# Three weight folds on TensorE in split fp32r products instead of f32, with the splitting on ScalarE and GpSimd

## The reference

```
Q = (x @ Wq), K = (ctx @ Wk), V = (ctx @ Wv)      # per batch, 8 heads of 256
score = Q K^T / sqrt(256); masked; attn = softmax(score)
out = (attn V) @ Wo + x
(out - mean) * rsqrt(var + 1e-5) * gamma + beta
```

## Time and profile before

| | us |
|---|---|
| median of 3 runs | 312.84 (312.39 to 313.38) |
| profiled execution | 312.59 |
| its span | 310.8 |
| TensorE busy | 304.6 |
| VectorE busy | 243.9 |
| ScalarE busy | 228.2 |
| GpSimd busy | 201.2 |
| granted clock | 1.00 |

### The profile page before, as it was taken

One profiled execution on the slowest core, in us unless ns is written; L12 is line 12 of the kernel. 1 busy time (PEld: TensorE's weight loads), 2 busy tenths in 40 slices (PEclk: granted clock), 3 DMA queues, 4 the chain that ended last, 5 costly groups with the idle time before them and its releaser, 6 DMA issues.

```text
span 310.8 us, 8035 instructions
## 1 busy us (share of the span) xinstructions
PE 304.6 (98%) x2570; PEld 298.0 (96%) x2570; DVE 243.9 (78%) x696; ACT 228.2 (73%) x615; POOL 201.2 (65%) x209
## 2 busy tenths in 40 slices
PE   8999999999999999999999999999999999999994
PEld 6898888999999999999999999999999999999994
DVE  0457778778998779787989879877988889877676
ACT  2546678768888687878887887868797797868760
POOL 1123476556868588857868487858878487857811
PEclk9999999999999999999999999999999999999999
DMA  7996444473354644574346543474455444543301
GB/s 248 367 404 257 138 137 153 144 218 114 95 167 144 208 154 135 175 249 139 114 147 190 185 148 118 164 232 135 135 172 181 155 141 147 166 149 124 84 2 68
DMA packets 48143, 51.32 MB, mean 165 GB/s; under 512 B 3584, under 2 KB 38144, under 8 KB 48128
## 3 DMA queue, kind: packets, MB, share of 16 engines
q1 hardware_dynamic: 47840, 50.61, 49.2%
q10 hardware_dynamic: 288, 0.52, 0.6%
HBM read 32.77 MB, written 18.35 MB: 164 GB/s over the span
## 4 chain that ended last, share of the span: by engine, by line
PE 96%; DMA 2%; DVE 1%; SPq 0%; POOLq 0%; issue 0%; POOL 0%
PE score_bank L346 25%; PE out_bank L346 19%; PE gL_bank L346 14%; PE tL_bank L346 13%; PE tU_bank L346 9%; PE gU_bank L346 7%; DMA wq_raw<-in_wqT 2%; PE spare_bank L346 1%; PE spare_bank L380 1%; PE tL_bank L380 1%; PE tL_bank L362 1%; PE tU_bank L362 1%; PE out_bank L386 1%; PE tU_bank L386 1%; PE spare_bank L362 0%; PE out_bank L362 0%
## 5 line engine op out<-in xcount | busy, mean ns | idle before, releaser
L1055 POOL TENSOR_TENSOR probs<-probs,inv_sum 128x512 f32<-128x512 f32 x64 | 66.7, 1043 | 63.1 <-DVE inv_sum L859 62.8
L651 ACT ACTIVATE probs<-neg_scores,neg_max 128x256 f32<-128x256 f32 x128 | 64.1, 502 | 32.3 <-DVE neg_max L848 32.3
L1098 POOL TENSOR_TENSOR pT_lo<-pT_raw,pT_hi 128x512 fp32r<-128x512 f32 x62 | 79.3, 1302 | 10.0 <-ACT pT_hi L607 10.0
L848 DVE CUSTOM_DVE_ANT_0 neg_scores<-score_bank,mask_bias 128x256 f32<-128x256 f32 x128 | 49.2, 422 | 6.7 <-PE score_bank L346 4.2
L869 DVE STREAM_TRANSPOSE squares<-probs 128x512 f32<-128x512 f32 x62 | 43.8, 706 | 0.3
L794 DVE TENSOR_TENSOR tL_lo<-tL_bank,tL_hi 128x512 fp32r<-128x512 f32 x30 | 20.8, 692 | 23.9 <-ACT tL_hi L607 23.9
L607 ACT ACTIVATE tL_hi<-tL_bank 128x512 fp32r<-128x512 f32 x30 | 17.9, 598 | 24.7 <-PE tL_bank L346 24.5
L607 ACT ACTIVATE pT_hi<-pT_raw 128x512 fp32r<-128x512 f32 x62 | 35.4, 623 | 0.0
L346 PE MATMUL gL_bank<-xT_hi,A_lo 128*128 128x256 f32 x128 | 35.3, 276 | 0.0
L346 PE MATMUL gL_bank<-xT_hi,A_hi 128*128 128x256 f32 x128 | 35.3, 276 | 0.0
L346 PE MATMUL gL_bank<-xT_lo,A_hi 128*128 128x256 f32 x128 | 35.3, 276 | 0.0
(11 more groups left out here) (192 smaller groups left out, 1010.7 us busy)
## 6 DMA issues: line engine op xcount, KB each, us to landing
scratch<-squares SPq DMA_DIRECT2D x31, 512.0 KB, 2.6
pT_raw<-scratch SPq DMA_DIRECT2D x124, 128.0 KB, 3.1
xT_raw<-in_xT SPq DMA_DIRECT2D x8, 256.0 KB, 3.2
ctxT_raw<-in_ctxT SPq DMA_DIRECT2D x8, 256.0 KB, 3.5
wo_raw<-in_wo SPq DMA_DIRECT2D x4, 512.0 KB, 14.8
x_res<-in_x SPq DMA_DIRECT2D x8, 256.0 KB, 3.0
out<-y SPq DMA_DIRECT2D x7, 256.0 KB, 2.7
wq_raw<-in_wqT SPq DMA_DIRECT2D x3, 512.0 KB, 7.6
```

Source lines behind the costliest of these rows:

```text
L651: nc.scalar.activation(probs[j % 2][:, n, :], neg_scores[:, n, :], ACT.Exp, bias=neg_max[:, n:n + 1], scale=-1.0, accum_out=row_sum[:, n:n ...
L848: nc.vector.tensor_tensor_reduce(out=neg_scores[:, n, :], in0=score_bank[hh][:, q, :], in1=mask_bias[:], scale=-SCALE, scalar=3.0e38, op0= ...
L1055: nc.gpsimd.tensor_tensor(probs[j % 2][:, rows, :], probs[j % 2][:, rows, :], inv, ALU.mult) \
L1098: nc.gpsimd.tensor_tensor(pT_lo[j % 2][:, k].rearrange("p hh (q i r) -> p (hh q) i r", q=QT, i=ROWS), pT_raw[j % 2][:, k].rearrange("p i n ...
```

## The change

The lower rows of fold 0 stay in f32. For pairs 1 to 3, wo (two heads, 128x512 each) and the lower 128 columns of wv (two heads, 128x256 each) are split into hi and lo: four ScalarE copies and four GpSimd subtractions a pair. They go into buffers that are idle at the time. The fold of the lower rows is 12 fp32r matmuls and stands behind the upper rows, which stay in f32; ScalarE and VectorE take the upper part first as well. SyncE's load of ctx moves from before the wv and wo loads to behind those of pair 1.

```diff
+        def wo_split(j, hh):
+            if j < PAIRS - 1:
+                return pT_hi[j - 1][:, hh], pT_lo[j - 1][:, hh]
+            return (gL_hi[:], gL_lo[:]) if hh == 0 else (gU[:], tL_hi[:])
+        def wv_split(j, hh):
+            if j < PAIRS - 1:
+                return by_half(CL_hi[:, 2 * j + 2 + hh, :]), by_half(CL_lo[:, 2 * j + 2 + hh, :])
+            return by_half(tL_lo[:, hh, :]), by_half((tU_hi, tU_lo)[hh][:])
+        def weight_parts(j, n):
+            tiles = slice((2 * j + n % 2) * DT, (2 * j + n % 2 + 1) * DT)
+            if n < 2:
+                return (wo_raw[:, tiles, :],) + wo_split(j, n)
+            return (wv_raw[:, tiles, 0:P],) + wv_split(j, n - 2)
...
@@ SyncE
-            load_ctx(0)
             for j in range(PAIRS):
                 ...
                 sp.dma_start(wo_raw[:, tiles], wo[:, tiles]).then_inc(o_weights_in[j], 16)
+                if j == 1:
+                    load_ctx(0)
@@ TensorE, fold_C (the f32 lower rows only for j == 0; the upper rows, then)
+                if j > 0:
+                    pe.wait_ge(weights_split, 4 * j)
+                    for hh in range(2):
+                        (v_hi, v_lo), (o_hi, o_lo) = wv_split(j, hh), wo_split(j, hh)
+                        pairs = []
+                        for d in range(DT):
+                            pairs += [(v_hi[:, d, :], o_hi[:, d, :]), (v_hi[:, d, :], o_lo[:, d, :]),
+                                      (v_lo[:, d, :], o_hi[:, d, :])]
+                        ins = split_products(lower[:, hh, :], pairs)
+                    ins.then_inc(C_product, 1)
@@ ScalarE
+            def weights_hi_part(j, n):
+                act.wait_ge(o_weights_in[j], 32)
+                raw, hi, _ = weight_parts(j, n)
+                hi_part(hi, raw).then_inc(weights_hi_done, 1)
...
+                if isinstance(t, int) and t == 0:
+                    weights_hi_part(1, 0)
+                    weights_hi_part(1, 1)
                 exponentials(t, j, heads=[0])
+                if isinstance(t, int) and t == 0:
+                    weights_hi_part(1, 2)
+                    weights_hi_part(1, 3)
                 ...
                 exponentials(t, j, heads=[1])
                 ...
                 for pair in folds:
                     C_hi_part(pair)
+                if isinstance(t, int) and t in (0, 1):
+                    for n in range(4):
+                        weights_hi_part(t + 2, n)
@@ GpSimd
+            def weights_lo_part(j, n):
+                pool.wait_ge(weights_hi_done, 4 * (j - 1) + n + 1)
+                raw, hi, lo = weight_parts(j, n)
+                lo_part(lo, raw, hi).then_inc(weights_split, 1)
...
+                if isinstance(t, int) and t == 0:
+                    weights_lo_part(1, 0)
+                    weights_lo_part(1, 1)
                 normalise_probs(t, j)
+                if isinstance(t, int) and t == 0:
+                    weights_lo_part(1, 2)
+                    weights_lo_part(1, 3)
+                    weights_lo_part(2, 0)
+                    weights_lo_part(2, 1)
                 if isinstance(t, int) and t == 1:
+                    weights_lo_part(2, 2)
+                    weights_lo_part(2, 3)
                     ctx_lo_part(b)
+                    weights_lo_part(3, 0)
+                if isinstance(t, int) and t == 2:
+                    weights_lo_part(3, 1)
+                    weights_lo_part(3, 2)
+                    weights_lo_part(3, 3)
                 ...
                 if j == 2 and not (isinstance(b, int) and b == B - 1):
                     xT_lo_part(b + 1)
```

More of the change, by code:

```diff
@@ L141, in attention_kernel, with pair_tiles, by_half @@
         pT_banks = [gL_bank, gU_bank]
+        def pair_tiles(j):
+            return slice(2 * j * DT, 2 * (j + 1) * DT)
+        def by_half(rows):
+            return rows.rearrange("p (d c) -> p d c", d=DT)
+        def wo_split(j, hh):
[11 more added lines that the diff above has]
+            return (wv_raw[:, tiles, 0:P],) + wv_split(j, n - 2)
         def places(name, t):
@@ L173, in attention_kernel @@
         A_split = sem("A_split")
+        weights_hi_done = sem("weights_hi_done")
+        weights_split = sem("weights_split")
         C_product = sem("C_product")
@@ L376, in fold_C @@
                 lower, upper = fold_C_banks(j)
[L377 to L382, removed]
+                if j == 0:
+                    for hh in range(2):
+                        h = 2 * j + hh
+                        for d in range(DT):
+                            ins = nc.tensor.matmul(lower[:, hh, :], wv_raw[:, h * DT + d, 0:P],
+                                                   wo_raw[:, h * DT + d, :], start=d == 0, stop=d == DT - 1)
+                    ins.then_inc(C_product, 1)
                 for hh in range(2):
@@ L622, in C_hi_part @@
                 act.wait_ge(C_product, 2 * j + 1)
-                hi_part(CL_hi[:, 2 * j:2 * j + 2, :], lower[:]).then_inc(C_hi_done, 1)
-                act.wait_ge(C_product, 2 * j + 2)
+                if j == 0:
+                    hi_part(CL_hi[:, 2 * j:2 * j + 2, :], lower[:]).then_inc(C_hi_done, 1)
+                    act.wait_ge(C_product, 2 * j + 2)
                 hi_part(CU_hi[:, j, :], upper[:, 0, :]).then_inc(C_hi_done, 1)
+                if j > 0:
+                    act.wait_ge(C_product, 2 * j + 2)
+                    hi_part(CL_hi[:, 2 * j:2 * j + 2, :], lower[:]).then_inc(C_hi_done, 1)
+            def weights_hi_part(j, n):
+                act.wait_ge(o_weights_in[j], 32)
+                raw, hi, _ = weight_parts(j, n)
+                hi_part(hi, raw).then_inc(weights_hi_done, 1)
             def ctxT_hi_part(b):
@@ L809, in C_lo_part @@
                 dve.wait_ge(C_hi_done, 2 * j + 1)
-                lo_part(CL_lo[:, 2 * j:2 * j + 2, :], lower[:], CL_hi[:, 2 * j:2 * j + 2, :]).then_inc(C_split, 1)
-                dve.wait_ge(C_hi_done, 2 * j + 2)
+                if j == 0:
+                    lo_part(CL_lo[:, 2 * j:2 * j + 2, :], lower[:], CL_hi[:, 2 * j:2 * j + 2, :]) \
+                        .then_inc(C_split, 1)
+                    dve.wait_ge(C_hi_done, 2 * j + 2)
                 lo_part(CU_lo[:, j, :], upper[:, 0, :], CU_hi[:, j, :]).then_inc(C_split, 1)
+                if j > 0:
+                    dve.wait_ge(C_hi_done, 2 * j + 2)
+                    lo_part(CL_lo[:, 2 * j:2 * j + 2, :], lower[:], CL_hi[:, 2 * j:2 * j + 2, :]) \
+                        .then_inc(C_split, 1)
             def lower_mask(b):
```

## The result

The changed kernel takes 313.88 us (median of 8 runs, 313.36 to 315.13), the kernel before 312.77 (8 runs): a ratio of 1.0037, interval 1.0022 to 1.0053. Slower, as forecast, but by 1.1 us where the forecast had 2.25 (2.3 on the median). The profiled execution took 313.88 with a span of 312.1, against 312.59 and 310.8: 1.3 us, nearly all of it there by the start of step 4's scores.

A forecast was written before the change was run, and what follows sets the result against it. TensorE, 98% busy, bounds the kernel, with VectorE's g loop and GpSimd's list close behind. Terms +1.92 - 0.44 + 0.27 - 0.44 + 0.55 - 0.44 + 0.83 = +2.25 us gave 314.84 profiled, 315.1 median; range 312.8 to 316.3.

The forecast's parts named there:

- the first stall: TensorE before step 1's scores: stands still 1.92 us, waiting for g delayed by the weight transfer; 0 to 2.4 by landing.
- the fold's saving: Lower fold on TensorE in steps 1 to 3: twelve fp32r matmuls in 1.38 us instead of 1.82, saving 0.44 each.
- step 1 with its fold, to step 2's scores: TensorE in step 1: fold saves 0.44 us, but VectorE's loop holds step 2's scores, giving back 0.27.
- step 2, to step 3's scores: TensorE in step 2: fold saves 0.44 us, but VectorE's loop holds step 3's scores, costing 0.55.
- wait for xT: Step 3's query products wait 0.83 us for xT's lower part, behind three weight parts on GpSimd in step 2.
- rest of step 3 with its fold: TensorE in step 3, apart from the xT wait: fold saves its full 0.44 us.
- This brings it 0.5 us forward: 22.0: Landing of pair 1's wo: moving ctx behind it brings it from 22.52 to 22.0 us; bounds 19.0 to 22.5.
- a first exponential before 22: Sign that would break the forecast, on ScalarE in step 0; the forecast had the first exponential near 23.0 us.
- would make 1.5: Pricing the twelve fold matmuls from the score products, 0.125 us apiece, gives 1.5 us; the forecast took 1.38.
- the loop holds there, as forecast: VectorE's g loop, periods 7.25 then 7.49 us, doesn't shrink with the fold; until step 3 TensorE can win only 0.24.
- Nothing is given back: From step 4's scores on TensorE sets the pace, so the whole +2.25 us stays to the end.
- the clock falls in the stall: Rival: TensorE, standing 1.92 us before step 1, drops to 1.2 GHz, costing up to 6.9 us more, 322; chance 0.03.

The follow-up runs named there:

- the changed kernel's second profile: The changed kernel run again unchanged, for the spread of the weight landing; 313.84 us, ratio 1.0032 to the kernel before; the profiled execution took 314.47.
- the two kernels with its order on ScalarE: Changed kernel with xT's lower part ahead of step 2's three weight parts on GpSimd: 313.29 us; changed kernel with f32 folds, splitting kept: 317.24, 314.10, 323.40, 323.86 us.
- the three kernels with the new order: Changed kernel, splitting parts spread over gaps, no weight wait before step 0's exponentials: xT late 314.63 us; xT first 312.51; xT early, lower rows first 312.51.
- the kernel with the folds alone: Kernel before without splitting; lower rows of folds 1 to 3 as fp32r matmuls on A's parts, upper rows first: 312.23 us, ratio 0.9986.
- the kernel with ctx first: Changed kernel with only the ctx load moved back ahead of all wv and wo loads: 315.73 us, ratio 1.0112 to the kernel before.
- The new order with xT late: Changed kernel with splitting parts spread over gaps, no weight wait before step 0's exponentials, xT still behind other parts in step 2: 314.63 us, ratio 1.0078.
- Two kernels: Kernel before, no splitting, fp32r folds 1 to 3 lower rows first: 321.39 us; the same with xT's parts as fold 1's moving operands: 321.67 us.
- Three kernels next to them: Fp32r folds without splitting, upper rows first: 312.23 us; only fold 3 upper rows first: 312.29; new splitting order, xT early, lower rows first in every fold: 312.51.

## Why the prediction was wrong in size

The direction, both stalls and their places were right; the size of the first stall and the fold's saving were not. The steps, in the time by which they move step 4's scores:

| step of the sum | predicted | measured |
|---|---|---|
| start of the stretch (wait for wq) | 0 | +0.10 |
| stall at step 1's scores | +1.92 | +0.51 |
| step 1 with its fold, to step 2's scores | -0.17 | -0.13 |
| step 2, to step 3's scores | +0.11 | +0.01 |
| wait for xT | +0.83 | +0.86 |
| rest of step 3 with its fold | -0.44 | -0.07 |
| sum | +2.25 | +1.28 |

1. *The step that failed is the landing.* "This brings it 0.5 us forward: 22.0" is the term that was mis-sized: the transfer landed at 20.58, 1.9 us forward and outside the 21 to 22.5 that the forecast was given for, and the first stall was 0.51 us instead of 1.92. The prediction's own sign says so too: a first exponential before 22 would break it, and it came at 21.67. The other traces give the spread. With ctx behind, the changed kernel's second profile and the two kernels with its order on ScalarE landed at 21.24, 21.53 and 22.17, the three kernels with the new order at 20.2 each; all seven are 20.9 in the mean, the first four 21.4. With ctx ahead it was 22.52, 22.3, 21.9, 22.3, 22.6 and 22.46, 22.4 in the mean. So moving 192 KB is worth 1.0 to 1.5 us in the mean and 1.9 between the two like kernels' profiles, whose medians differ by 1.8, not the 0.5 of its bytes. Within one group the landings differ by 0.7 to 2 us. The changed kernel's two runs at 314.93 and 315.13 lie where landings of 21.6 and 21.8 would put them; they have no profile. Why a transfer of 0.5 us holds another up for longer is open; with 256 KB more ahead it landed no later (22.53). The Trainium skill ("DMA: Bandwidth & Descriptors", Why a DMA increments its semaphore by 16 and not by 1) has the engines of a transfer finish independently and the semaphore full only with the last of them. These landings, 1 to 3 us behind the count of bytes, are compatible with it, but no trace here shows the engines one by one.
2. *What followed from the landing was right.* From landings 20.58, 21.24, 21.53, 22.17, 22.46 and 22.53 the scores of step 1 came at 26.66, 27.29, 27.59, 28.22, 28.50 and 28.58. That is 6.04 to 6.08 us behind each; the forecast had 27.97 - 22.0 = 5.97.
3. *The fold's saving was mis-sized, by more than half.* 0.44 a fold was predicted; the kernel with the folds alone gained 0.57 for three, 0.19 each. By start times the whole fold with its change of stage took 2.75 and 2.64 us in steps 1 and 3 against 2.84, and of the 2.75 another 0.10 is the wait for gU. I had priced it from the query products at 0.113 us. The prediction had the better row in hand, the score products that "would make 1.5", and took 1.38; it was 1.54. These operands run at 0.12 (+0.08), and the first product behind the 64-column f32 matmuls takes 0.22 instead of 0.12 (+0.10); some 0.1 more is lost in entering the upper rows right behind the query products. In the 41.30 - 33.91 = 7.39 us of step 2 nothing is won at all: its end follows 0.15 us behind gU's lower parts of step 3 (40.27 + 0.88 = 41.15 on VectorE), so the loop holds there, as forecast, and holds the end of step 1 too (33.77 to 33.91). In step 3, where the gain should have counted in full, the fold is 0.20 shorter, but the 18 query products, now started behind a wait, take 2.24 us instead of 2.04 and use it up; only the context products are 0.07 faster.
4. *The wait for xT was right*, place and size: 0.86 against 0.83.
5. *"Nothing is given back"* held: 1.28 us at step 4, 1.3 at the end.
6. Two errors had opposite signs and in part cancelled, which was luck: -1.4 for the landing, +0.4 for step 3 (the last row but one of the table). With the measured landing the prediction's sum gives 0.8, with ctx first 2.7, where 1.28 and 3.1 were measured; the difference of 0.4 both times is for the most part the saving that step 3 didn't have.
7. The rival "the clock falls in the stall" had 0.03. It didn't decide the changed kernel, but it is real: with stalls of 2.08 and 2.46 us the clock fell to 0.50 (1.2 GHz) in both profiles. With 2.44 us, in the kernel with ctx first, it stayed at 1.00 in the profile, while another execution of that kernel had a mean of 0.986 and 318.62 us. The new order with xT late, with a stall of 2.0 us, had two of six runs near 316.1 with a mean clock of 0.992, where the others took 314.6. So a stall of this length sometimes costs the clock and sometimes doesn't. The Trainium skill ("TensorE: Matmul & The Clock Gate", Part 1) has an idle array put back to half rate; two of these three profiles agree, the third doesn't show it.

## What to carry to other kernels

Taking work from the engine that is 98% busy by giving more to its neighbours paid here only where each new part stood behind the instruction that this engine waits for next: the same splitting cost 1.1 us in one order and gained 0.26, if anything, in another. Price the shorter work from the row with the most similar operands and the same neighbours, not from the fastest row. A new wait at the head of an in-order list for something that before was merely early (pair 1's weights landed at 22.5 and were first read at 30.6) turns that transfer's spread into the kernel's. Price a landing from several executions, and a changed order of loads by a test, not by bytes.

## What the runs showed of the hardware

- TensorE's pace for a 128x256 fp32r product at full clock isn't one number: 0.113 us with A's parts (stationary) against xT, 0.12 with A against A or CL against pT, 0.1175 for the query products behind a wait (12 in 1.41 us). The score products take 0.12 while g lies in g_early (20 in 2.38 to 2.39 us) and 0.113 from step 5 on, when it lies in gL and gU (20 in 2.27).
- Two kernels ran the entire loop at 0.1175 instead of 0.113 us a product, 8.6 us in all, at granted clock 1.00 and in all of their nine runs, after a change of three short folds ahead of it. Three kernels next to them did not. Not operands, not the order of folds 1 and 2, not lower rows first in fold 3 by itself; the cause is open.
- A stall of TensorE of a little over 2 us cost 1.1 and 1.5 us more through the clock in two profiles (the twenty score products behind it took 3.75 and 4.08 us instead of 2.62) and nothing in a third.
